# Row maxima for an attention step: one 32-row transfer and four small transposes in place of eight transfers and one transpose

## What is computed

```python
q = (xn @ q_w + q_b).reshape(Bx, Tx, H, -1)
k = (xn @ k_w + k_b).reshape(Bx, Tx, H, -1)
att = jnp.einsum('bnhl,bmhl->bnmh', q, k)
att = att + (1.0 - mask) * -1000000.0
att = jax.nn.softmax(att, axis=2)
y = jnp.einsum('bnmh,bmhl->bnhl', att, v).reshape(Bx, Tx, Dx)
h = layer_norm(y, sb_norm_w, sb_norm_b) * (1.0 + scale) + shift
h = jax.nn.silu(h) @ out_w + out_b
return x + h
```

## Time and profile before

| what | value |
|---|---|
| median of 3 runs | 1525.5 us (1525.44 to 1538.27) |
| profiled execution, its own time | 1538.5 us |
| its span, first to last instruction | 1536.7 us |
| mean granted clock of TensorE | 0.929 |
| PE / DVE / ACT / POOL busy | 90% / 68% / 47% / 49% |
| layer 1's attention, first `a` to last step | about 539 to 1507 us |

### The profile page before, as it was taken

One profiled execution on the slowest core, in us unless ns is written; L12 is line 12 of the kernel. 1 busy time (PEld: TensorE's weight loads), 2 busy tenths in 40 slices (PEclk: granted clock), 3 DMA queues, 4 the chain that ended last, 5 costly groups with the idle time before them and its releaser, 6 DMA issues.

```text
span 1536.7 us, 28241 instructions
## 1 busy us (share of the span) xinstructions
PE 1379.5 (90%) x10808; PEld 1105.5 (72%) x10808; DVE 1037.4 (68%) x2035; ACT 717.0 (47%) x1291; POOL 750.2 (49%) x673
## 2 busy tenths in 40 slices
PE   8899999999999889788888888988988888898978
PEld 5788888888887756666767676766777667676656
DVE  5888787887888756675466457556647646755754
ACT  4444545544555245355345345535534534543643
POOL 0324424424425236575468348557456636854732
PEclk9999999999999989898899889998899989998989
DMA  8012112021142675454354344436236335443412
GB/s 311 28 35 90 30 61 80 31 69 63 39 125 83 193 219 168 120 142 125 111 140 137 100 133 128 137 99 179 85 118 170 108 111 139 132 125 105 149 26 83
DMA packets 88423, 173.95 MB, mean 113 GB/s; under 512 B 12744, under 2 KB 12744, under 8 KB 88288
## 3 DMA queue, kind: packets, MB, share of 16 engines
q1 hardware_dynamic: 88288, 172.15, 37.1%
HBM read 104.45 MB, written 67.14 MB: 112 GB/s over the span
## 4 chain that ended last, share of the span: by engine, by line
PE 63%; DVE 15%; SPq 11%; DMA 5%; issue 3%; ACT 2%; POOL 1%; DVEq 0%; ACTq 0%
PE ps L542 11%; PE ps L544 11%; PE ps L543 11%; PE ps L709 10%; SPq L1615 9%; DVE cT L1225 7%; PE ps L701 6%; PE ps L762 5%; PE ps L537 3%; DMA Qs<-nxT 3%; PE ps L714 2%; DVE ps L1192 1%; PE ps L651 1%; PE ps L630 1%; DVE nxT L1246 1%
## 5 line engine op out<-in xcount | busy, mean ns | idle before, releaser
L1412 POOL TENSOR_TENSOR Pb<-Pb 128x512 f32<-128x512 f32 x360 | 450.1, 1290 | 367.6 <-PE ps L762 367.6
L1225 DVE TENSOR_REDUCE cT<-ps 128x1 f32<-128x512 f32 x512 | 329.2, 684 | 260.5 <-PE ps L701 260.0
L959 ACT ACTIVATE Pb<-ps 128x512 f32<-128x512 f32 x512 | 274.8, 603 | 343.9 <-PE ps L709 322.6
L709 PE MATMUL ps<-Qs,Ks 100*128 100x512 f32 x512 | 220.2, 512 | 127.5 <-DMA Qs<-nxT 127.4
L709 PEld LDWEIGHTS ps<-Qs,Ks 100*128 100x128 f32 x512 | 125.0, 251 | 178.6 <-issue 147.3
L701 PE MATMUL ps<-Ks,Qs 98*128 98x512 f32 x512 | 189.1, 423 | 6.9 <-DMA Ks<-stack_scratch 3.0
L1334 POOL TENSOR_TENSOR rs<-ve,mhalf 128x4 f32<-128x4 f32 x32 | 33.1, 1033 | 221.8 <-DVE ve L1045 153.7
L701 PEld LDWEIGHTS ps<-Ks,Qs 98*128 98x128 f32 x512 | 99.2, 199 | 42.2 <-DVE cT L1225 7.6
L542 PE MATMUL ps<-xTh,Wh_k 128*128 128x512 f32 x256 | 111.3, 435 | 5.3 <-DVE Wl_k L998 2.9
L542 PE MATMUL ps<-Wh_o,sTh 128*128 128x512 f32 x256 | 106.9, 418 | 2.1 <-DVE sTl L1203 2.1
L544 PE MATMUL ps<-xTh,Wl_k 128*128 128x512 f32 x256 | 106.0, 414 | 0.0
(11 more groups left out here) (175 smaller groups left out, 2919.9 us busy)
## 6 DMA issues: line engine op xcount, KB each, us to landing
Qs<-stack_scratch SPq DMA_DIRECT2D x32, 768.0 KB
Ks<-stack_scratch SPq DMA_DIRECT2D x32, 768.0 KB
stack_scratch<-sg_q SPq DMA_DIRECT2D x32, 512.0 KB, 2.7
stack_scratch<-sg_k SPq DMA_DIRECT2D x32, 512.0 KB, 3.1
wr<-in_x SPq DMA_DIRECT2D x32, 256.0 KB, 4.4
x_scratch<-wr SPq DMA_DIRECT2D x32, 256.0 KB, 2.0
stack_scratch<-sg_q SPq DMA_DIRECT2D x32, 256.0 KB, 3.0
stack_scratch<-sg_k SPq DMA_DIRECT2D x32, 256.0 KB, 3.6
```

The lines of the kernel that those rows point to most:

```text
L709: e.matmul(bank[:], Ks[par][0:RE, j, m * 128:(m + 1) * 128], Qs[par][0:RE, j, :], start=True, stop=True).then_inc(s["ST"], 1)
L959: e.activation(p_buf(n, m)[:, j, :], ps[bank_of["a", n, m, j]][:], ACT.Exp).then_inc(s["P"], 1)
L1225: e.tensor_reduce(nx[:, n % 2, j, t, 0:1], ps[bank_of["S", n, j, t]][:], AX.X, ALU.max, negate=True).then_inc(s["S_max"], 1)
L1412: e.tensor_tensor(acc[:, j, :], acc[:, j, :], p_buf(n, m)[:, j, :], ALU.add).then_inc(s["Ps_pool"], 1)
```

## The change

`nxs` shrinks to 32 columns: 16 for the high parts and 16 for the low parts, each in the order (j, t). The three reductions work on the same numbers in that order. In place of one transpose of 128x128, four transposes of 32x32 put quarter u of the partitions to columns 32u of `nxT`, which now is 32 rows of 128. So a row of `nxT` is one contiguous piece of 128 tokens of a row of `Qs`, and one DMA of 32 rows replaces the eight. The waits count 16 where they counted 128. Nothing else changes: the row sums are still made by POOL's adds and the selector products.

```diff
-        nxs = sb("nxs", [128, NT, 32], FR)
-        nxT = sb("nxT", [128, NT * 32])
+        nxs = sb("nxs", [128, 32], FR)
+        nxT = sb("nxT", [32, 128])
...
-                    e.wait_ge(s[f"nxq{par}"], 128 * (n // 2 + 1))
+                    e.wait_ge(s[f"nxq{par}"], 16 * (n // 2 + 1))
...
-                    m = nx[:, n % 2].rearrange("p j t s -> p t j s")
-                    hi = nxs[:, :, 0:4]
+                    m = nx[:, n % 2].rearrange("p j t s -> p (j t) s")
+                    hi, lo = nxs[:, 0:16], nxs[:, 16:32]
...
-                    e.transpose(nxT[:], nxs[:].rearrange("p t c -> p (t c)").bitcast(F32)).then_inc(s["nx_tr"], 1)
+                    for u in range(4):
+                        r = e.transpose(nxT[:, 32 * u:32 * u + 32], nxs[32 * u:32 * u + 32, :].bitcast(F32))
+                    r.then_inc(s["nx_tr"], 1)
...
-                    for u in range(4):
-                        for r in range(2):
-                            row = Qs[par][RX + r:RX + r + 1, :, :].rearrange("p j (t n) -> p j t n", t=NT)[:, :, :, 32 * u:32 * u + 32]
-                            src = nxT[32 * u + 4 * r:32 * u + 4 * r + 4, :].rearrange("j (t n) -> j t n", t=NT)
-                            e.dma_start(row.bitcast(F32), src).then_inc(s[f"nxq{par}"], 16)
+                    e.dma_start(Qs[par][RX:RE, :, :].bitcast(F32).rearrange("s j (t n) -> s (j t) n", t=NT),
+                                nxT[:]).then_inc(s[f"nxq{par}"], 16)
```

More of the change, by code:

```diff
@@ L1236, in nxt @@
                     e.wait_ge(s["S_max"], 16 * n + 16)
-                    e.tensor_reduce(hi, m[:, :, :, 0:1], AX.X, ALU.max).then_inc(s["nx_hi"], 1)
+                    e.tensor_reduce(hi, m[:, :, 0:1], AX.X, ALU.max).then_inc(s["nx_hi"], 1)
                     e.wait_ge(s["nx_hi"], n + 1)
-                    e.tensor_reduce(m[:, :, :, 1], hi.bitcast(F32).unsqueeze(3), AX.X, ALU.max, negate=True).then_inc(s["nx_neg"], 1)
+                    e.tensor_reduce(m[:, :, 1], hi.bitcast(F32).unsqueeze(2), AX.X, ALU.max, negate=True).then_inc(s["nx_neg"], 1)
                     e.wait_ge(s["nx_neg"], n + 1)
                     with nc.allow_low_precision(reason="the sum of a number and its negated high part is exact"):
-                        e.tensor_reduce(nxs[:, :, 4:8], m, AX.X, ALU.add).then_inc(s["nx_lo"], 1)
+                        e.tensor_reduce(lo, m, AX.X, ALU.add).then_inc(s["nx_lo"], 1)
                     if n:
-                        e.wait_ge(s[f"nxq{(n - 1) % 2}"], 128 * ((n - 1) // 2 + 1))
+                        e.wait_ge(s[f"nxq{(n - 1) % 2}"], 16 * ((n - 1) // 2 + 1))
                     e.wait_ge(s["nx_lo"], n + 1)
-                    e.transpose(nxT[:], nxs[:].rearrange("p t c -> p (t c)").bitcast(F32)).then_inc(s["nx_tr"], 1)
+                    for u in range(4):
+                        r = e.transpose(nxT[:, 32 * u:32 * u + 32], nxs[32 * u:32 * u + 32, :].bitcast(F32))
+                    r.then_inc(s["nx_tr"], 1)
             def tl(i, n):
```

## The result

The kernel after takes 1364.16 us (median of 4 runs, 1360.68 to 1366.31) against 1526.68 us for the kernel before (4 runs, 1525.44 to 1538.27). The ratio is 0.892, with a 95% interval of 0.887 to 0.897. The profiled execution of after took 1360.7 us, that of before 1538.5: this pair differs by 177.8 us, the medians by 162.5.

A forecast was written before the change was run, and what follows sets the result against it. PE was taken as the bound, busy 1379.5 of 1536.7 us, its `Qs<-nxT` wait costing idle time and then half clock. Wait 112.3 plus clock 74.2 make 186.5 us; 1525.5 less that is 1339 us, range 1315 to 1415.

The forecast's parts named there:

- Eight issues to one: SP's transfers from `nxT` to `Qs`: seven issues go, the one left lands in 2.1 us, gaining 4.3 us a step.
- One transpose to four: DVE's transposes before the transfer: four small ones in place of one add 0.3 us a step, bounds 0 and 0.43.
- What is left of PE's wait: PE's wait for `Qs<-nxT`: with landings 4.0 us earlier, 9.7 us remain, plus 5.4 us from DVE's lateness.
- DVE late in kind 0: DVE at `sg_q` becomes 0.9 us late and delays the maxima and next `a`: six steps, 5.4 us.
- POOL: POOL's adds in steps of kind 1: its slack of 6.97 us just covers PE moving up 6.6 us, staying hidden.
- The clock: PE's heads after the wait return to full clock: 28 heads gain 2.65 us each, 74.2 us in all.
- When the clock falls: PE's clock in the heads: it fell after long waits and not after two short ones of 2.41 and 2.56 us.
- The base: The saving of 186.5 us, subtracted from the profiled 1538.5 us, gives 1352; from the median 1525.5 us, 1339 us.
- A: Rival: PE's waits go but its clock stays low, 1413 us; chance 0.12.
- B: Rival: DVE and POOL become the bound, 14 steps each lose 3 us more, 1381 us; chance 0.14.
- C: Rival: the single transfer lands as late as the old ones, at 6.1 us, 1525 us, no change; chance 0.04.
- D: Rival: the single transfer queues behind other loads and lands in 8.4 us, giving 1600 us; chance 0.04.

The follow-up runs named there:

- e5: The kernel after, unchanged, measured again beside new runs of the kernel before: 1361.8 us, ratio 0.885 to the kernel before.
- e6: The kernel after with two transfers of 16 rows a step in place of one of 32: 1367.9 us, ratio 0.889 to the kernel before.
- e3: The kernel after with its layout and four transposes, but eight transfers of 4 rows a step: 1539.8 us, ratio 1.002 to the kernel before.
- e4: The kernel after with its layout and four transposes, but four transfers of 8 rows a step: 1423.8 us, ratio 0.927 to the kernel before.
- e2: The kernel before with 14 dummy matmuls of 512 columns on PE ahead of its wait for the transfers, output unchanged: 1473.3 us, ratio 0.958.
- e8: The kernel after with the `nxt` work placed earlier on DVE in steps of kind 0: 1367.0 us, ratio 0.889 to the kernel before.
- e1: The kernel before, unchanged, run again for a profile near its median: 1535.9 us, ratio 0.9996.

## Why the prediction was right, and where it was off

Forecast 1339 us with a range of 1315 to 1415; measured 1364, or 1362 in e5. The two main terms, the wait and the clock behind it, were right in mechanism, and the chance of 0.92 for faster was well placed. A smaller term, DVE's lateness, was not, and the forecast of what would be left of the wait came true by luck. By its own steps:

- **Eight issues to one.** Landing taken at 2.1 us, measured 2.22 in step 16 and 2.18 in the median step. Right. A transfer of 32 rows lands 0.5 us later than one of four rows did (1.68). In the trace its 32 pieces run in two streams side by side, one piece every 23 ns in each, and end with two 4-byte completion writes, while a 16-row transfer of e6 has 16 such writes and landed after 1.85. The Trainium skill has the rule that the prediction quoted ("DMA: Bandwidth & Descriptors", section "Why a DMA increments its semaphore by 16 and not by 1"), by which this shape runs on two queues, and the trace agrees. The landings differ by 0.37 us, less than an issue takes; e6's transfer also has half the rows, so the queues' own share of it is not shown.
- **Issue time beside the transfer.** e3, e4, e6 and e5 (eight, four, two, one) took 1540, 1424, 1368 and 1362 us. An issue took SP 0.57 to 0.64 us in the median of each of these runs, against landings of 1.6 to 2.2 us, and SP makes them one after another. The Trainium skill ("DMA: Bandwidth & Descriptors", section "Issuing engines are not separate DMA queues") calls the time to initiate a DMA usually small relative to the DMA itself; the runs disagree for these transfers of 2 to 16 KB.
- **One transpose to four.** Taken at +0.3 us, inside bounds of 0 and 0.43; measured 0.85 - 0.31 = +0.54, above the upper bound. The nearest row, a reduction of 186 ns, was the right guide for one transpose (200 ns), but four in a row also leave 13 ns between them, and the value taken should have been the sum and not a point below it. Price: up to 0.24 us in each of the 22 steps in which PE still waits, some 5 us in all. With both terms together the landing comes 6.76 - 3.13 = 3.63 us earlier after the transposes begin (the earlier trace rows and step 16 above), where 4.0 was forecast.
- **What is left of PE's wait.** Forecast "about 15", from 9.7 and 5.4; measured 15.3. The agreement is luck. 2.32 us stand in step 0, 1.25 in step 1, 4.04 in step 3, 0.70 to 0.76 in the steps of kind 1 from 4 to 27, where 3.4 / 6 + 0.9 = 1.5 was forecast, and 0.20 to 0.28 in most of kinds 0 and 3, where nothing was. Nearly all of it is the old wait less the 3.65 us or so by which the landing moved: 5.99 gives 2.34, 7.70 gives 4.05, 4.43 gives 0.78, 3.92 gives 0.27. With each step's own landings it comes out to within 0.06 us in all 32 steps, step 1 included, whose transfer took 4.54 us to land. So 0.35 us too much taken off every wait stood against a lateness that did not come. The idle time gone, 112.7 by the page and 111.5 by e2 and e5, stands against 112.3.
- **DVE late in kind 0.** This term, 0.9 us in six steps or 5.4 us, is the one whose mechanism did not show. DVE's `sg_q` operation, which idled 5.66 us, indeed has no idle before it now. But the maxima do not come later for PE. In step 17, before, the transposes start at 1065.10, PE stops at 1067.59 and the rows land at 1071.87; after, it is 970.98, 973.50 and 974.06. PE reaches its wait 2.5 us behind the transposes in both kernels, and the wait is shorter by what the landing is (lines below). The maxima do stand 5.0 us behind the last row maximum there, in both kernels, and e8 shows that the wait goes when they don't.
- **POOL.** It kept 1.01 us before the adds of kind 1, where about 0.4 was forecast (the 6.6 there contains 0.8 us for which it gives no row). Hidden, as said.

The transposes, the landing and the wait of step 17, before:

```profile
1065.10 0.32 DVE nxT L1246
...
1070.18 1.69 DMA Qs<-nxT
...
1072.01 0.76 PE L709 MATMUL ps<-Qs,Ks 100*128 100x512 f32 x1 [4.42 <-DMA Qs<-nxT]
```

The same after, with `sg_q` on DVE ahead of them and POOL's adds behind:

```profile
954.71 0.74 DVE L1217 SCALAR_TENSOR_TENSOR sg_q<-ps,cols,sg_q 128x512 fp32r<-128x512 f32 x1
...
970.98 0.20 DVE nxT L1247
...
971.90 2.16 DMA Qs<-nxT
...
974.20 0.93 PE L709 MATMUL ps<-Qs,Ks 100*128 100x512 f32 x3 [0.70 <-DMA Qs<-nxT]
...
980.87 5.02 POOL L1414 TENSOR_TENSOR Pb<-Pb 128x512 f32<-128x512 f32 x4 [1.01 <-PE ps L762]
```

- **The clock.** Here a term was mis-sized: 28 heads by 2.65 = 74.2 us forecast, 65 measured (65.1 by PE's busy time, 66 by e2). The 24 heads of steps 4 to 27 gained 2.51 us each: 2.7 in kind 0, 2.8 in kind 2, 2.5 in kind 3, but 2.0 in kind 1. Steps 0, 28 and 31 gained 2.5, 3.0 and 1.5, step 30 only 0.3 (its clock falls in after too, 0.78), and the head of step 3 became 0.9 us longer, since its clock still falls behind a wait of 4.04 us (0.68 over the head). I had applied one price to heads that differ. Step 1, which the prediction left out, had a fallen clock as well (0.87) and gained 2.8 us of PE's busy time. By busy time the heads gain 69.4 us in all; 0.9 came back before step 0 and 3.4 behind the heads, 0.1 to 0.2 us in most steps.
- **When the clock falls.** The prediction read the two short waits of 2.41 and 2.56 us, after which the heads ran at 1.00, as a sign that the clock falls after long waits alone. The other two of the four short ones say otherwise: the head after the wait of 2.98 us (1418.90 in the earlier trace rows) ran at 0.72, by the line below, and that of step 1, after 2.58 us, at 0.87. The length of the wait did not sort even the trace of before. The gain came all the same, because the change took the waits away almost wholly.

```profile
1418.90:1430.78 11.88, 11.88 (x94) 9.32 (x94) 7.30 (x16) 7.83 (x14) 1.99 (x3) 0.72 0.46 169
```

- **The base.** The last step, subtracting from the median of 1525.5, was the larger error. The 25 us between 1339 and 1364 are 13 of base, 8.7 of the sum and 3.5 by which the median of after lies above its profiled execution. Sum against the profiled execution: 1352 forecast, 1360.7 measured, off by 8.7, which is the clock's 9.1 less 0.4 of idle time. The terms had been read from an execution of 1538.5 us, which had more half-clock time than one of 1525 can have had, and part of the 186.5 us may have existed only there. In e5 before took 1539 and after 1362, as on the first occasion: the saving is larger where before is slower, which fits a change that removes what makes before vary. That an execution at 1525 has less half-clock time fits the runs of e1, but no profile of one was taken.
- **The rivals.** A (clock stays low) fell: 0.99 from 538 us on, and e2 recovers 66 us by filling the wait. B fell: between 538 and 1327 us PE idled 21.0 us, 13.0 of it for `Qs<-nxT`, so 8.0 is left for all other names together, against the 25 that B asked. C and D fell: the landing is 2.2 us, not 6.1.

## What to carry to other kernels

When the chain of waits shows an engine's queue that only issues small transfers, count the issues between the last input and the last landing, since each moved the landing by 0.55 to 0.69 us here. What a halving brings has to be read as first issue to last landing, not as a number of issues: 5.94, 3.82, 2.41 and 2.18 us gave 116, then 56, then 6 us. A wait of PE must be priced twice, as idle time and as the stretch at half clock that may follow it, and both prices are visible separately on the page, as idle and as busy time of PE. What is left of a wait can be worked out as the old wait less the shift of what ends it, step by step; here that gives every rest to 0.06 us. Take a saving worked out from a profiled execution against that execution, and if its time is not the median's, ask which of its terms makes the difference.

## What was not expected of the hardware

- The clock's cost can be had back without touching the wait: 14 matmuls whose result nobody uses, 3.36 us of PE in a time that it would mostly have idled through, took the kernel before from 1539 to 1473 us.
- A wait of 1.86 or 1.88 us is followed in one step by a clock of 0.76 over the head and in another by 1.00 (e4). Waits of 2.3 to 2.7 us in another kind of step left it at 1.00 five times in six. I had taken a wait of under 2 us to be safe.
- Four transposes of 32x32 that touch different partitions don't overlap: 0.20 us each, one every 0.21 us. One transpose of 128x32 does the four's work on DVE in 0.211 us.
- An issue of four rows cost SP 0.623 us with pieces of 128 bytes and 0.573 with pieces of 512 (e3). One of 32 rows, eight times the payload, cost 0.617 (after). Those of 8 rows cost 0.635 (e4) and those of 16 rows 0.586 (e6), so the issue time hardly follows the payload.
